# Router logits with the router matrix as the stationary operand, in four 32-column strips

## What is computed

```python
x = x + 0.5 * ffn(layernorm(x))      # routing 1, experts 1
x = x + attn(layernorm(x))           # a linear attention with a cumulative sum
x = x + 0.5 * ffn(layernorm(x))      # routing 2, experts 2

def ffn(x):                          # E = 32 experts, C = 640 slots each
    logits = xt @ w_router           # [16384, 256] @ [256, 32]
    probs = softmax(logits); top1 = argmax(probs); gate = probs[top1]
    pos = cumsum(onehot(top1))[top1] - 1          # place in the expert's queue
    slot = where(pos < C, top1 * C + pos, E * C)  # else dropped
    y = (silu(buf @ w_gate) * (buf @ w_up)) @ w_down
    return xt + where(accepted, y[slot] * gate, 0)
```

## Time and profile before

| what | us |
|---|---|
| median of 3 runs | 1724.47 |
| profiled execution, its own time | 1724.29 |
| its span, first to last instruction | 1722.5 |
| PE / PEld busy | 1465.6 / 1416.1 |
| DVE / ACT / POOL busy | 1145.1 / 1103.7 / 861.4 |
| mean granted TensorE clock, share of full | 0.908 |

### The profile page before, as it was taken

How to read it: one execution, slowest core, us unless ns; L and a number is a source line. 1 busy time by engine, 2 the same in 40 slices (tenths; PEclk the granted TensorE clock), 3 DMA queues, 4 the chain that set the end, 5 groups by cost and what they waited for, 6 DMA issues and landing times. The chain is left out here.

```text
span 1722.5 us, 32675 instructions
## 1 busy us (share of the span) xinstructions
PE 1465.6 (85%) x10850; PEld 1416.1 (82%) x10850; DVE 1145.1 (66%) x2961; ACT 1103.7 (64%) x2324; POOL 861.4 (50%) x1149
## 2 busy tenths in 40 slices
PE   4766760899999999389999999999925999999997
PEld 4655650899999999389999999999925999999996
DVE  3534530677777777367778878877824777777775
ACT  4656760666666666268777777777714666666664
POOL 3277776244443434234346667666772343434343
PEclk9656655899999999799999999999967999999999
DMA  9996542666666667320122222211113444444541
GB/s 363 379 307 214 190 160 93 201 225 215 197 225 222 203 209 241 117 67 27 60 86 62 90 82 68 82 63 41 63 45 119 121 119 136 140 136 118 151 135 34
DMA packets 196854, 250.09 MB, mean 145 GB/s; under 512 B 24618, under 2 KB 181976, under 8 KB 192592
## 3 DMA queue, kind: packets, MB, share of 16 engines
q1 hardware_dynamic: 169040, 204.23, 37.3%
q0 software_dynamic: 27648, 43.78, 7.3%
HBM read 128.05 MB, written 152.17 MB: 163 GB/s over the span
## 5 line engine op out<-in xcount | busy, mean ns | idle before, releaser
L800 PE MATMUL ps<-xs,ws 128*128 128x320 f32 x3072 | 464.4, 310 | 0.0
L800 PEld LDWEIGHTS ps<-xs,ws 128*128 128x128 f32 x3072 | 454.7, 189 | 0.6 <-issue 0.6
L280 POOL DMA_INDIRECT slots<-xn,r x256 | 258.6, 1010 | 107.4 <-issue 97.5
L800 PE MATMUL ps<-ws,hs 128*128 128x256 f32 x1920 | 275.3, 291 | 28.1 <-DVE hs L721 28.1
L631 POOL DMA_INDIRECT x_rows<-ys,oidx x160 | 169.0, 1056 | 250.2 <-DVE ys L742 220.3
L631 POOL DMA_INDIRECT out<-ys,oidx x160 | 168.5, 1053 | 249.6 <-DVE ys L742 219.8
L800 PEld LDWEIGHTS ps<-ws,hs 128*128 128x128 f32 x1920 | 241.0, 190 | 41.1 <-DVE hs L721 41.1
L757 DVE TENSOR_TENSOR hf<-ps,sg 128x320 f32<-128x320 f32 x256 | 125.7, 491 | 164.1 <-ACT sg L685 164.0
L654 ACT CAST xs<-ps 128x512 fp32r<-128x512 f32 (+1 forms) x192 | 99.6, 520 | 160.0 <-PE ps L793 160.0
L707 DVE TENSOR_TENSOR ws<-wraw,ws 128x512 fp32r<-128x512 f32 x192 | 132.6, 692 | 82.6 <-ACT ws L647 79.5
L301 ACT ACTIVATE xn<-x,r 128x256 f32<-128x256 f32 x256 | 138.8, 591 | 66.2 <-DMA slots<-xn,r 37.4
(11 more groups left out here) (108 smaller groups left out, 2632.7 us busy)
## 6 DMA issues: line engine op xcount, KB each, us to landing
slots<-zero SPq DMA_DIRECT2D x32, 1300.0 KB, 10.2
xg<-slots SPq DMA_DIRECT2D x64, 650.0 KB
x<-in_x SPq DMA_DIRECT2D x32, 512.0 KB, 6.0
x_rows<-x SPq DMA_DIRECT2D x32, 512.0 KB, 3.6
wraw<-in_w_gate SPq DMA_DIRECT2D x64, 256.0 KB, 2.8
wraw<-in_w_up SPq DMA_DIRECT2D x64, 256.0 KB, 3.2
wraw<-in_w_down SPq DMA_DIRECT2D x64, 256.0 KB, 3.8
x<-x_rows SPq DMA_DIRECT2D x32, 512.0 KB, 5.2
```

What stands on the lines that cost most here:

```text
L280: nc.gpsimd.indirect_dma_start(out=self.slots, out_offset=bass.IndirectOffsetOnAxis(ap=self.slot[:, t % XR, k:k + 1], axis=0), in_=self.xn ...
L800: ins = pe.matmul(dst, left(a, k), right(b, k), start=(n == 0), stop=(n == len(terms) - 1))
```

## The change

The router matrix half (128x32) becomes the stationary operand and the turned rows of four tiles (two units, p = n // 2) are moved, 128 columns each: tile i goes to column strip i, so its 32 logits for 128 tokens lie on PSUM partitions 32i to 32i + 31 of a "raw" bank (`pe_raw`). ACT copies that 128x128 block to SBUF (`act_keep`), and one PE transpose of it brings four tiles' logits back with tokens on the partitions, in the place where they stood before (`pe_logits`). The raw bank is bank 6 in `route`; in `attention` it is bank 7, shared with `sums` and the count, which wait for each other's readers. `xt` holds four tiles twice instead of two tiles twice. All lags behind the logits grow: in `route` POST 9 to 11 and SCATTER 13 to 15; in `attention` posts 0 to 2 and the count by one, with the count moved from the end of step 18 to the head of step 19, where it now also waits for copies. The rstd rings (`rb`, `nb`, `ve`, `mn`, `s1`, `s2`) go from 2 to 3 batches, and the waits for them from t-1 to t-2.

```diff
-                self.rb, self.nb, self.ve, self.mn = (s([P, 2, TB]) for _ in range(4))
-                self.s1, self.s2 = s([P, 2, TB]), s([P, 2, TB])
+                self.rb, self.nb, self.ve, self.mn = (s([P, XR, TB]) for _ in range(4))
+                self.s1, self.s2 = s([P, XR, TB]), s([P, XR, TB])
-                self.xt = s([P, 2, HC, CH, P])
+                self.xt = s([P, 2, HC, 2 * CH, P])
+                self.lt = s([P, 2, P])
...
-                    pool.wait_ge(self.ready.sem, self.ready.at(t - 1))
-                    pool.wait_ge(self.normed.sem, self.normed.at(NC * (t - 1)))
-                    pool.wait_ge(self.based.sem, self.based.at(NC * (t - 1)))
+                    pool.wait_ge(self.ready.sem, self.ready.at(t - 2))
+                    pool.wait_ge(self.normed.sem, self.normed.at(NC * (t - 2)))
+                    pool.wait_ge(self.based.sem, self.based.at(NC * (t - 2)))
...
             def act_evac(self, act, n):
+                p, o = n // 2, n % 2 * CH
                 act.wait_ge(self.turned.sem, self.turned.at(n + 1))
-                act.wait_ge(self.logits.sem, self.logits.at(n - 1))
-                act.copy(self.xt[:, n % 2].rearrange("p a b c -> p (a b c)"),
-                         ps[:, self.bt[n % len(self.bt)], :]).then_inc(self.evac.sem, 1)
+                act.wait_ge(self.raw.sem, self.raw.at(p - 1))
+                act.copy(self.xt[:, p % 2, :, o:o + CH, :],
+                         ps[:, self.bt[n % len(self.bt)], :].rearrange("p (a b c) -> p a b c", a=HC, b=CH)
+                         ).then_inc(self.evac.sem, 1)
+
+            def act_keep(self, act, p):
+                act.wait_ge(self.raw.sem, self.raw.at(p + 1))
+                act.wait_ge(self.logits.sem, self.logits.at(p - 1))
+                act.copy(self.lt[:, p % 2, :], ps[:, self.br, 0:P]).then_inc(self.kept.sem, 1)
...
-            def pe_logits(self, pe, n):
-                t = n // NC
-                pe.wait_ge(self.evac.sem, self.evac.at(n + 1))
-                if n % NC == 0:
+            def pe_raw(self, pe, p):
+                pe.wait_ge(self.evac.sem, self.evac.at(2 * p + 2))
+                pe.wait_ge(self.kept.sem, self.kept.at(p))
+                for h in range(HC):
+                    for i in range(2 * CH):
+                        ins = pe.matmul(ps[E * i:E * i + E, self.br, 0:P], WR[:, h, :], self.xt[:, p % 2, h, i, :],
+                                        start=(h == 0), stop=(h == HC - 1))
+                ins.then_inc(self.raw.sem, 1)
+
+            def pe_logits(self, pe, p):
+                t = 2 * p // NC
+                pe.wait_ge(self.kept.sem, self.kept.at(p + 1))
+                if 2 * p % NC == 0:
                     pe.wait_ge(self.shifted.sem, self.shifted.at(t + 1 - len(self.bl)))
-                for j in range(CH):
-                    k = CH * n % TB + j
-                    for h in range(HC):
-                        ins = pe.matmul(ps[:, self.bl[t % len(self.bl)], k * E:(k + 1) * E],
-                                        self.xt[:, n % 2, h, j, :], WR[:, h, :], start=(h == 0), stop=(h == HC - 1))
-                ins.then_inc(self.logits.sem, 1)
+                o = 2 * p % NC * CH * E
+                pe.transpose(ps[:, self.bl[t % len(self.bl)], o:o + P], self.lt[:, p % 2, :],
+                             IDENT).then_inc(self.logits.sem, 1)
...
-                LEAD, POST, SCATTER, BASE = 4, 9, 13, 3
+                LEAD, POST, SCATTER, BASE = 4, 11, 15, 3
...
+                        if S % 2 == 1 and 0 <= S - 3 < NU:
+                            tail.act_keep(act, (S - 3) // 2)
...
-                        if 0 <= S - 1 < NU:
-                            tail.pe_logits(pe, S - 1)
+                        if S % 2 == 0 and 0 <= S - 2 < NU:
+                            tail.pe_raw(pe, (S - 2) // 2)
+                        if S % 2 == 0 and 0 <= S - 4 < NU:
+                            tail.pe_logits(pe, (S - 4) // 2)
...
-                POST_AT, COUNT_AT, SCATTER_AT, BASE_AT = (14, 15, 16, 19), 18, 20, 7
+                POST_AT, COUNT_AT, SCATTER_AT, BASE_AT = (15, 16, 17, 19), 19, 20, 7
...
+                        for n in at(S, LOGIT):
+                            if n % 2 == 1:
+                                tail.act_keep(act, n // 2)
...
                         pe.wait_ge(gram_read.sem, gram_read.at(a + 1))
+                        if a >= 1:
+                            pe.wait_ge(tail.kept.sem, tail.kept.at(4 * a - 3))
...
                     for S in range(FIRST, LAST):
+                        for t in batches(S, COUNT_AT):
+                            if t + 2 < BATCH:
+                                pe.wait_ge(sums_read.sem, sums_read.at(t + 3))
+                            pe.wait_ge(tail.kept.sem, tail.kept.at(min(4 * t + 6, NU // 2)))
+                            tail.pe_count(pe, t)
...
+                        for n in at(S, LOGIT + 1):
+                            if n % 2 == 1:
+                                tail.pe_logits(pe, n // 2)
                         for n in at(S, LOGIT):
-                            tail.pe_logits(pe, n)
+                            if n % 2 == 1:
+                                for a in batches(S, 2):
+                                    pe.wait_ge(sums_read.sem, sums_read.at(a + 1))
+                                for t in batches(S, COUNT_AT + 1):
+                                    pe.wait_ge(tail.cread.sem, tail.cread.at(t + 1))
+                                tail.pe_raw(pe, n // 2)
```

More of the change, by code:

```diff
@@ L168, in macaron, with __init__ @@
         class Tail:
-            def __init__(self, stack, tag, turn_banks, logit_banks, count_bank, groups, stream, slots):
-                self.bt, self.bl, self.bc = turn_banks, logit_banks, count_bank
+            def __init__(self, stack, tag, turn_banks, logit_banks, count_bank, raw_bank, groups, stream, slots):
+                self.bt, self.bl, self.bc, self.br = turn_banks, logit_banks, count_bank, raw_bank
                 self.groups, self.stream, self.slots = groups, stream, slots
@@ L193, in __init__ @@
                 self.scaled = count(f"{tag}_scaled")
-                self.normed = count(f"{tag}_normed", NC + 1)
-                self.based = count(f"{tag}_based", NC + 1)
+                self.normed = count(f"{tag}_normed", 2 * NC + 1)
+                self.based = count(f"{tag}_based", 2 * NC + 1)
                 self.turned = count(f"{tag}_turned")
                 self.evac = count(f"{tag}_evac", 2)
+                self.raw = count(f"{tag}_raw_logits", 2)
+                self.kept = count(f"{tag}_raw_kept", 1)
                 self.logits = count(f"{tag}_logits", 2)
@@ L205, in __init__ @@
                 self.carried = count(f"{tag}_carried")
-                self.ready = count(f"{tag}_slots", 2)
+                self.ready = count(f"{tag}_slots", 3)
                 self.total = sem(f"{tag}_total")
@@ L318, in act_base @@
                     x_t = self.stream.tile(CH * n + j)
-                    ins = act.activation(x_t, x_t, ACT.Identity, bias=self.s2[:, t % 2, k:k + 1],
-                                         scale=self.s1[:, t % 2, k:k + 1])
+                    ins = act.activation(x_t, x_t, ACT.Identity, bias=self.s2[:, t % XR, k:k + 1],
+                                         scale=self.s1[:, t % XR, k:k + 1])
                 ins.then_inc(self.based.sem, 1)
@@ L328, in pe_setup @@
                 self.logits.grant(pe)
+                self.raw.grant(pe)
             def pe_turn(self, pe, n):
@@ L386, in post @@
                 if step == 0:
-                    dve.wait_ge(self.logits.sem, self.logits.at(NC * t + NC))
+                    dve.wait_ge(self.logits.sem, self.logits.at(NC // 2 * (t + 1)))
                     dve.reduce_max(mx, lg, AX).then_inc(links.sem, 1)
@@ L399, in post @@
                 if step == 2:
[L400 to L401 removed]
+                    dve.tensor_tensor(std, self.ve[:, t % XR, :], self.rb[:, t % XR, :], ALU.mult)
+                    dve.tensor_scalar(row[:, :, R_B], self.mn[:, t % XR, :], -1.0, None, ALU.mult)
                     dve.tensor_copy(row[:, :, R_ID].bitcast(U32), TOK[:, TB * t:TB * t + TB])
@@ L441, in route @@
                     groups += [(NC * t + lo, NC * t + lo + w) for lo in range(0, NC, w)]
-                tail = Tail(st, "p1", (0, 1), (2, 3), 4, groups, stream, slots1)
-                LEAD, POST, SCATTER, BASE = 4, 9, 13, 3
+                tail = Tail(st, "p1", (0, 1), (2, 3), 4, 6, groups, stream, slots1)
+                LEAD, POST, SCATTER, BASE = 4, 11, 15, 3
                 s_const = sem("const_in")
@@ L495, in _ @@
                     tail.based.grant(act)
-                    for S in range(NU + 12):
+                    for S in range(NU + 14):
                         for t in batches(S, POST + 2):
@@ L509, in _ @@
                     tail.dve_setup(dve)
-                    for S in range(-LEAD, NU + 13):
+                    for S in range(-LEAD, NU + 15):
```

(6 more changed lines are left out.)

9 lines of the change are left out of this document (4 added, 5 removed).

## The result

The changed kernel takes 1708.26 us (median of four runs, 1706.37 to 1709.49) against 1723.54 us of the kernel before (median of four too): 0.991 of it, 95% interval 0.9893 to 0.9927. The time moved by -15.3 us where -7 was forecast. It lies inside the range. The profiled execution took 1709.49 us.

What follows compares the result with a forecast made beforehand. PE was taken to bound attention until batch 5, POOL its end and routing. Attention's pairs -10.4, count +1.0, POOL's wait -2.2 and routing +4.5 summed to -7.1 us: 1717 us, range 1702 to 1742.

Steps and rivals of the forecast that it cites:

- What bounds the stages: Attention bound by PE, 100% busy, until batch 5 is ready, then by POOL; routing bound by POOL.
- The strips: Attention's eight logits matmuls per pair of steps, partly overlapping: 1.0 us, between 0.44 and 1.78, replacing 1.62.
- all four at once: Rival, chance 0.15: attention's strips fully overlap, 0.44 us; a pair gains 0.96, kernel 1705 us.
- the waits of the count: Attention's count waiting for ACT's copy: +1.0 us in step 58; 0.4 us each batch if strips took 0.44.
- POOL's wait: At attention's end, the wait of 2.17 us for group 60 disappears in full: -2.2 us, between 0 and -2.2.
- The estimate by the Trainium skill's speedup of three column tiles: Attention's strips priced by a 2.38 times speedup: 0.75 us a pair, 1711 us for the kernel.
- The change of mode: Attention, PE switching from whole array to strips and back: 0.10 us a pair, between nothing and 0.33.
- The turn back: Attention, one PE turn of the copied 128x128 tile per pair: 0.12 us added.
- the cover of 5.6: Attention's tail: last batch's slots ready 5.6 us before POOL needs them, hiding 1 to 2 us of later logits.
- Routing: Routing stage lengthened by new POOL waits before groups 32, 40, 48: +4.5 us, between -4 and +8.
- the lags cost: Routing: scatters two steps later put each rstd four scatters (5.1 us) earlier on POOL, so it waits for inputs.
- the gain is given back: Rival, chance 0.13: mode change costs 0.33 a pair, routing's waits +4 to +6; 1722 to 1726 us.

Runs made afterwards that it cites:

- the four runs: Changed kernel (1820.52 us, second chip) with strip matmuls ordered by strip, on one strip, on two strips, or issued twice: 1821.05, 1852.09, 1828.71, 1839.86 us.
- routing_long_lags: Changed kernel with routing's strips taken out, each step's logits by themselves, longer lags kept (posts 11, scatters 15): 1703.71 us, 0.9883 of the kernel before.

## Why the prediction was right or wrong

**What bounds the stages** held: PE in attention until batch 5, POOL behind it and in routing.

**The strips** were the term mis-sized. The step that failed reads: "two records of one matmul share a strip and follow each other, so only the second of one strip can lie beside the first of the next". They do share it, but the other strips don't wait behind them; the price is the fullest strip's, four records, and 0.12 us. It measured 0.57 us for my 1.0, at the lower bound of 0.44 and a little more. The rival that I gave 0.15, all four at once, was the mechanism; its result of 1705 is 3.3 us below the measured one: a pair gained 0.91 for its 0.96 (1.3 us), the waits of the count took 6.2 for its 3.6 (2.6), the 2.2 us of POOL's wait brought nothing, and routing lost 2.7 less. The estimate by the Trainium skill's speedup of three column tiles (TensorE: Matmul & The Clock Gate, Measured speedup vs the span model), 0.75 us and 1711 us, was nearer than mine; the table there names no data type, so that they are bf16 was my reading. The Trainium skill's page TensorEngine Tiling (Array Packing), Key Properties, says that tiles operate independently: by the four runs, the traces agree.

**The change of mode** I took at 0.10 us. Delta's twelve records take 1.59 us to the next start ahead of strips (1054.78 to 1056.37) and 1.50 ahead of the turn back; 0.07 to 0.09, and what is fixed within the 0.57. The rule of that section of the Trainium skill, that changing the mode drains TensorE, is neither shown nor excluded; what it can cost here is at most some 0.2 us together, less than the upper bound of 0.33. **The turn back** was 0.11 for 0.12. A pair gains 0.91 us where 0.40 stood.

**The waits of the count** were under-priced. The forecast had +1.0 in step 58 alone and, if the strips were fast, 0.4 a batch. Measured: 0.70 in each of four batches, 1.87 ahead of batch 5's count, and 1.5 more for the count at the low clock: 6.2 us. The step that failed is "PE meanwhile has strips 1.0, turns and gram 1.78 (1069.77 to 1071.55): 2.78, no wait": it rests on the strips' own mis-sized term, 0.43 us, and on a copy done 2.65 us after delta's end. ACT's timeline has the copy's end 3.15 us after it (1056.37), since softplus ends later:

```profile
1059.27 0.25 ACT L320 COPY r<-ps 128x128 f32<-128x128 f32 x1
```

And no term allowed for a count at the low clock; that its 1.5 us go with the wait is not shown, since routing_long_lags has the wait without them.

**POOL's wait of 2.17 us** at the end of attention did go, as the prediction had it, and brought nothing: 90.3 us for 90.2. POOL's lines there, before and after, show where it went:

```profile
L272 POOL TENSOR_SCALAR x<-x,r 128x256 f32<-128x256 f32 x22 | 13.5, 624 | 0.4
```

```profile
L275 POOL TENSOR_SCALAR x<-x,r 128x256 f32<-128x256 f32 x22 | 16.1, 740 | 0.4
```

The 22 base operations, the first fence before and the second after, take 2.6 us longer; they now fall beside other work of DVE. Pairs of them that take 1.3 to 2.2 us instead of 1.1 overlap DVE's scans (L1080, now L1105) or the last operation of post 1 (L398, now L416): three before, five after. The mistake was to take the wait off and leave POOL's own work as it was. The last batch's slots were ready at 1257.3 + 0.2, some 5 us ahead of POOL, as the cover of 5.6 had it.

**Routing** was right in its parts and wrong in its sum. Waits of 5.28, 1.17 and 1.55 us came where 5.6, 1 to 1.5 and 1 were forecast; post 0 of batch 3 began at 149.09 (148.6), the aggregate at 155.43 (155.7, its end then). The first scatter stayed, 77.90. But the stage lost 1.8 us, not 4.5: against the 4.1 us of waits POOL's L255 took 19.2 us in all instead of 20.7, since three of its thirteen had run 0.4 to 0.5 us long beside DVE's L398, and the scatters 126.7 instead of 127.5. And the reason given, that the lags cost, was wrong: it is the strips' two steps of latency, 5.8 us; the lags without them gain 4.4. The prediction had both in one sum and so could not tell that the part of the change which was to help is the part that hurts here.

Together, on the first chip: attention -16.4 (forecast -11.6 with the wait), routing +1.8 (+4.5). That the whole is only 8 us off is in part luck: the pairs gave 13.3 us more than forecast, waits that I had at less or as gone took 7.4 back, and routing lost 2.7 less; some 1 us is left over. On the second chip the result of the rival *the gain is given back* came, no gain, but not its terms: the change of mode is as cheap there, and attention as short.

## What to carry to other kernels

Price column strips by the fullest strip, not by the order of issue, and check that they pay where TensorE is the bound: in routing, which another engine bounds, the same edit only added the latency of a pair, a copy and a turn, and cost 5.8 us. When a step on the bounding engine gets shorter, look again at every hand-over that was covered by it; moving one 0.25 us copy ahead of two long operations gave a third of the whole change's gain again. And time a change of 1% on more than one chip before believing its sign.

## What was not expected of the hardware

- Sixteen fp32 records of 128 moved columns take 1.87, 1.02 and 0.57 us on one, two and four strips; the records of one strip do not hold up those of another behind them (0.60 us with four in a row on each).
- Behind a stop of PE of 1.87 us ahead of a count the granted clock was 0.55 for the next 3.4 us in one trace and full in another with the same stop; behind stops of 0.55 and 0.70 us it stayed full.
- POOL's 22 base operations at the end of attention took 624 ns in one kernel and 740 in the other on the same work; the long ones overlap DVE's scans or the last operation of post 1.
- Chips of two speeds: the kernel before is 5% slower on one, the changed kernel 6.6%, with equal instruction times. Of the changed kernel's 111 us, 96.5 are time in which PE is idle (311.9 us against 408.4). The change's sign differs between the two.
